# A decoder layer with two attentions and experts: maxima turned as a product into spare columns, biases added to the residual, the usual arm of the branch in line

## The reference

```python
x = layernorm(x + attn(x))          # 16 heads of 8, one shared K and V of width 8
x = layernorm(x + xattn(x, ctx))    # 16 heads of 8, 6404 keys, each head its own K and V
x = layernorm(x + ffn(x))           # 8 experts, each token takes the best one

# attn:  softmax(Q K^T / sqrt(8)) V @ Wo + bo
# xattn: scores where mask == 0 are set to -1e9, softmax, V, @ Wo^T + bo
# ffn:   probs = softmax(x @ router^T + rb); e = argmax(probs)
#        y = (x @ expert_w[e]^T + expert_b[e]) * probs[e]
```

## Time and profile before

| | us |
|---|---|
| median of 3 runs | 573.07 (571.8 to 575.85) |
| the profiled execution | 574.0 |
| its span | 572.4 |
| TensorE busy | 512.7 (90%) |
| VectorE busy | 432.6 (76%) |
| ScalarE busy | 356.1 (62%) |
| POOL busy | 186.9 (33%) |
| mean granted TensorE clock | 0.945 of full speed |

### The profile page before, as it was taken

The page is one execution under the profiler, slowest core; times in us unless marked ns, Lnnn a source line. Parts: engine busy times, 40 slices in busy tenths (PEclk is TensorE's granted clock), DMA queues, the critical chain, the costliest instruction groups (busy, mean ns, idle before and its releaser), DMA issues.

```text
span 572.4 us, 13811 instructions
## 1 busy us (share of the span) xinstructions
PE 512.7 (90%) x4112; PEld 211.0 (37%) x4120; DVE 432.6 (76%) x640; ACT 356.1 (62%) x680; POOL 186.9 (33%) x297
## 2 busy tenths in 40 slices
PE   7998899989999997857899999999999999979981
PEld 2332233323333344622344444444444444327440
DVE  5998789889999733436888888888888888302667
ACT  6147678878888863150377777777777777860210
POOL 1135798898920000010233333333333333200000
PEclk9999889999999997886999999999999999995697
DMA  3389978775000013422233111111111111110001
GB/s 85 93 298 310 306 267 300 289 272 220 11 21 11 11 50 120 137 74 56 51 65 70 43 39 36 30 36 36 32 34 36 34 36 37 34 32 24 0 0 37
DMA packets 21770, 52.56 MB, mean 92 GB/s; under 512 B 5021, under 2 KB 13375, under 8 KB 19649
## 3 DMA queue, kind: packets, MB, share of 16 engines
q1 hardware_dynamic: 19037, 22.72, 14.7%
q0 software_dynamic: 2304, 28.84, 13.8%
q10 hardware_dynamic: 356, 0.10, 0.1%
HBM read 42.10 MB, written 8.94 MB: 89 GB/s over the span
## 4 chain that ended last, share of the span: by engine, by line
PE 73%; DVE 9%; ACT 6%; issue 6%; DMA 5%; ACTq 1%; SPq 0%; DVEq 0%
PE O L1166 25%; PE ST L1387 13%; PE ST L1197 9%; PE RT L1359 8%; DMA Qs<-mxr 4%; PE RT L1183 3%; DVE mxs L718 3%; PE RT L1489 2%; PE RT L1313 2%; PE RT L1312 2%; ACT prob L1007 2%; DVE x L906 1%; ACT prob L1044 1%; PE ST L1141 1%; PE RT L1092 1%
## 5 line engine op out<-in xcount | busy, mean ns | idle before, releaser
L863 DVE TENSOR_REDUCE mxc<-RT 128x1024 f32 (+1 forms) x192 | 198.3, 1046 | 33.5 <-PE RT L1359 28.6
L1044 ACT ACTIVATE prob<-ST 128x512 f32<-128x512 f32 x320 | 172.9, 592 | 47.1 <-PE ST L1387 45.1
L718 DVE TENSOR_REDUCE mxs<-RT 128x2 f32<-128x1024 f32 x128 | 152.9, 1223 | 19.1 <-PE RT L1183 16.8
L1007 ACT ACTIVATE prob<-ST 128x512 f32<-128x512 f32 x256 | 140.3, 597 | 37.4 <-PE ST L1197 29.6
L1359 PE MATMUL RT<-Kr,Qs 64*128 64x128 f32 (+1 forms) x512 | 122.9, 380 | 8.9 <-issue 7.9
L1387 PE MATMUL ST<-Qs,Kc 64*128 64x512 f32 x320 | 123.2, 454 | 1.1 <-DMA Qs<-mxr 0.7
L1197 PE MATMUL ST<-Qs,Kself 64*128 64x512 f32 x256 | 97.1, 463 | 10.5 <-DMA Qs<-mxr 5.3
L1166 PE MATMUL O<-prob,vst 128*9 128x256 f32 x1280 | 99.1, 381 | 0.6 <-ACT prob L1044 0.6
L1183 PE MATMUL RT<-Kself,Qs 64*128 64x512 f32 x256 | 94.1, 463 | 3.4 <-DVE mxs L718 1.5
L1166 PE MATMUL O<-prob,Vs 128*9 128x256 f32 x1024 | 80.3, 386 | 2.0 <-ACT prob L1007 0.8
L1359 PEld LDWEIGHTS RT<-Kr,Qs 64*128 64x128 f32 x512 | 60.2, 186 | 38.0 <-DVE mxc L863 24.6
(11 more groups left out here) (214 smaller groups left out, 390.6 us busy)
## 6 DMA issues: line engine op xcount, KB each, us to landing
big<-in_mask POOLq DMA_DIRECT2D x16, 1760.0 KB, 7.9
big<-kd SPq DMA_DIRECT2D x66, 80.0 KB
od_s<-osb SPq DMA_DIRECT2D x14, 128.0 KB, 3.0
od_x<-osb SPq DMA_DIRECT2D x14, 128.0 KB, 1.8
Qs<-qd_s SPq DMA_DIRECT2D x12, 128.0 KB, 4.0
Qs<-qd_x SPq DMA_DIRECT2D x12, 128.0 KB, 3.8
qd_s<-Vx SPq DMA_DIRECT2D x2, 512.0 KB, 4.0
qd_x<-big SPq DMA_DIRECT2D x2, 512.0 KB, 5.0
```

The source lines that it names most:

```text
L718: v.tensor_reduce(mxs[:, h % 2, c2, :].rearrange("p (f t) -> p f t", f=2)[:, :, q], RT[r % 2][:, :].rearrange("p (f k) -> p f k", f=2), AX ...
L863: v.tensor_reduce(o, src, AX.X, ALU.max).then_inc(S("x_row_free"), 1)
L1007: nc.scalar.activation(prob[:, c % SLOTS, k * HALF:(k + 1) * HALF], ST[(2 * c + k) % 3][:, :], ACT.Exp) \
L1044: nc.scalar.activation(prob[:, b, (k % 2) * HALF:(k % 2 + 1) * HALF], ST[BANK[k]][:, :], ACT.Exp) \
```

## The change

Several edits at once. `zrow` grows from 256 to 384 columns, `clear_o` clears 384 columns of `O`, and in both attentions, but for head 0, the maxima are turned by an ordinary product with the identity that adds to these zeros in columns 256 to 383. In self-attention this moves from block 4 to the start of block 2 of the head before; the wait for the copy moves to just before the block's value products:

```diff
             def turn_max(a, h, bank):
                 pe.wait_ge(S(a + "_mx_split"), h + 1)
+                if bank is None:
+                    mmul(O[0:16, 256:256 + P], mxh[:, :, :, :].bitcast(F32).rearrange("p f k t -> p (f k t)"),
+                         ident[:, :], start=False, stop=False, skip_group_check=True).then_inc(S(a + "_mx_turned"), 1)
+                    return
...
-                mmul(O[:, 0:256], zrow[:, 0:P], zrow[:, :], start=True, stop=False, skip_group_check=True)
+                mmul(O[:, 0:256 + P], zrow[:, 0:P], zrow[:, :], start=True, stop=False, skip_group_check=True)
...
-                turn = (c + 4) % SELF_U == 0 and (c + 4) // SELF_U < HEADS
+                turn = (c + 6) % SELF_U == 0 and (c + 6) // SELF_U < HEADS
+                if turn:
+                    turn_max("s", (c + 6) // SELF_U, None)
                 self_col(c, 0)
                 if r < HEADS * SELF_U:
                     self_row(r, 1)
-                if turn:
-
-                    pe.wait_ge(S("s_exp"), 2 * c - 1)
-                    turn_max("s", (c + 4) // SELF_U, (2 * c + 1) % 3)
-                    pe.wait_ge(S("s_mx_copied"), (c + 4) // SELF_U + 1)
                 self_col(c, 1)
                 if r < HEADS * SELF_U:
                     self_row(r, 0)
+                if turn:
+                    pe.wait_ge(S("s_mx_copied"), (c + 6) // SELF_U + 1)
...
                         if turn:
-
-                            pe.wait_ge(S("x_exp"), e + 4)
-                            turn_max("x", h_turn, BANK[7])
+                            turn_max("x", h_turn, None)
                         col(g, T, 2 * b, e + max(2 * b + 1 - AGAIN[2 * b], 0))
                         if h < HEADS:
                             rows(1, b - 1, h, U)
-                        if turn:
-                            pe.wait_ge(S("x_mx_copied"), h_turn + 1)
                         col(g, T, 2 * b + 1, e + (2 * b + 2 - AGAIN[2 * b + 1]))
                         if h < HEADS:
                             rows(0, b - 1, h, U)
+                        if turn:
+                            pe.wait_ge(S("x_mx_copied"), h_turn + 1)
```

ScalarE's copies move with them: of the maxima in self-attention to block 2, in cross-attention behind exponential 5 instead of 4; of `O` in cross-attention one exponential forward:

```diff
                 step_exp(T0, 0)
-                step_exp(T0, 1)
                 if g:
                     copy_o("x", g - 1, act.snap(T0 * NBLK + NBLK))
+                step_exp(T0, 1)
...
-                    if k == 4 and g + 1 < HEADS:
-                        max_copy("x", g + 1, BANK[7])
+                    if k == 5 and g + 1 < HEADS:
+                        max_copy("x", g + 1, None)
```

```diff
+            def add_bias(a):
+
+                k = "sx".index(a) + 2
+                dve.wait_ge(S("bias_rows"), k)
+                if a == "x":
+                    dve.wait_ge(S("s_x"), QT)
+                rows = (ST[2] if a == "s" else RT[1])[:, 0:D].unsqueeze(1).to_broadcast([P, QT, D])
+                v.tensor_tensor(x[:, :, :], x[:, :, :], rows, ALU.add).then_inc(S("bias_added"), 1)
+
+            def sums_back(a):
                 dve.wait_ge(S(a + "_o_back"), 16 * 15)
                 v.reciprocal(rden[:, :], den[:, :]).then_inc(S(a + "_rden"), 1)
...
-            dve.wait_ge(S("s_pv"), HEADS * SELF_U - 2)
-            with dve.Fori(0, n1) as i:
-                keys_of_pair(1, dve.snap(i + 1))
...
+            add_bias("s")
+            sums_back("s")
+            dve.wait_ge(S("s_pv"), HEADS * SELF_U)
+            with dve.Fori(0, n1) as i:
+                keys_of_pair(1, dve.snap(i + 1))
...
             def project_out(a, w):
                 pe.wait_ge(S("sel_made"), 1)
-                warm_up(ST[2], 8)
+                if a == "x":
+                    warm_up(ST[2], 16)
...
+                pe.wait_ge(S("bias_added"), "sx".index(a) + 2)
+                if a == "s":
+                    pe.wait_ge(S("x_k_f"), n)
+                    pe.wait_ge(S("x_k_hi"), n)
...
-                    mmul(RT[1][:, q * D:(q + 1) * D], orow[:, :], bo[a][:, :], start=True, stop=False, skip_group_check=True)
-                    mm = mmul(RT[1][:, q * D:(q + 1) * D], aT[:, q * P:(q + 1) * P], w[:, :], start=False, stop=True,
-                              skip_group_check=True)
+                    mm = mmul(RT[1][:, q * D:(q + 1) * D], aT[:, q * P:(q + 1) * P], w[:, :], start=True, stop=True)
```

The expert biases are made behind unit 5 instead of unit 3, second half first; ScalarE copies them to SBUF, POOL adds them to `x`, and VectorE waits for that (`bias_in`) before unit 8 and before the statistics, in place of its two adds:

```diff
+            for h in (1, 0):
+                w = slice(4 * h, 4 * h + 4)
+                pool.wait_ge(S("bias_copied"), 2 - h)
+                if h == 0:
+                    pool.wait_ge(S("f_sum"), 4 * E)
+                g_.tensor_tensor(x[:, w, :], x[:, w, :], be_rows[h], ALU.add).then_inc(S("bias_in"), 1)
```

More of the change, by code:

```diff
@@ L177, in decoder_layer @@
         kx_hi = [kx_ha, xroom[:, 0:PAIR].bitcast(F32R)]
+        be_rows = [prob[:, 3 + h, 0:HALF].rearrange("p (t d) -> p t d", d=D) for h in range(2)]
         outs = prob[:, 2, :].rearrange("p (t d) -> p t d", d=D)
@@ L278, in o_rows @@
                     return
+                load(den[g * DH:(g + 1) * DH, :], osb[DH:P:32, g % 2, :], a + "_o_back")
                 for q in range(4 if g == HEADS - 2 else 2):
@@ L401, in _ @@
             load(we, t["we"].rearrange("d (e o) -> d e o", e=E), "we_in")
-            for q in range(QT):
+            for q in range(0, QT, 2):
                 sp.wait_ge(S("out_done"), q + 1)
@@ L898, in _ @@
             for u in range(0, 2 * QT, 2):
+                if u == QT:
+                    dve.wait_ge(S("bias_in"), 1)
                 dve.wait_ge(S("y_all"), u + 2)
@@ L911, in _ @@
             dve.wait_ge(S("f_sum"), done)
-            for h in range(2):
-                dve.wait_ge(S("y_bias"), h + 1)
-                w = slice(4 * h, 4 * h + 4)
-                ch(v.tensor_tensor(x[:, w, :], x[:, w, :], (ST[0] if h else O)[:, :]
-                                   .rearrange("p (t d) -> p t d", d=D), ALU.add))
+            dve.wait_ge(S("bias_in"), 2)
             for h in range(2):
@@ L961, in max_copy @@
                     act.wait_ge(S(f"{a}_max_in{h % 2}"), 16 * (h // 2))
-                nc.scalar.copy(mxr[:, h % 2, :], ST[bank][0:16, 0:P]).then_inc(S(a + "_mx_copied"), 1)
+                turned = O[0:16, 256:256 + P] if bank is None else ST[bank][0:16, 0:P]
+                nc.scalar.copy(mxr[:, h % 2, :], turned).then_inc(S(a + "_mx_copied"), 1)
             def copy_o(a, g, pv):
@@ L1076, in _ @@
                 nc.scalar.copy(coefT[:, h * HALF:(h + 1) * HALF], ST[1 + h][0:E, :]).then_inc(S("coefT_copied"), 1)
+            for h in (1, 0):
+                act.wait_ge(S("y_bias"), 2 - h)
+                nc.scalar.copy(be_rows[h], (ST[0] if h else O)[:, :].rearrange("p (t d) -> p t d", d=D)) \
+                    .then_inc(S("bias_copied"), 1)
             act.preload_act_table(ACT.Sqrt)
@@ L1079, in _ @@
                 std("f", h)
+            for q in range(1, QT, 2):
+                act.wait_ge(S("out_done"), q + 1)
+                act.dma_start(out.rearrange("(t p) d -> p t d", p=P)[:, q, :], outs[:, q, :]).then_inc(S("stored"), 16)
         @block.tensor
@@ L1469, in cross @@
                 values(HEADS - 1, pe.snap(n * (HEADS - 1) + n1), NBLK - 1, n * (HEADS * NCOL))
-            pe.wait_ge(S("x_q_high"), 2)
-            pe.wait_ge(S("x_q_full"), 2)
-            pe.wait_ge(S("x_q0_z"), DIRECT)
-            with pe.If(general == 1):
-                cross(True)
-            with pe.Else():
-                cross(False)
-            project_out("x", wo_x)
-            pe.wait_ge(S("x_xT_copied"), 2)
-            for q in range(QT):
-                mm = mmul(ST[0][:, q * E:(q + 1) * E], xT[:, q * P:(q + 1) * P], wr[:, :], start=True, stop=True)
@@ new lines, in finish @@
+            def finish():
+                bias_rows("x")
+                project_out("x", wo_x)
+                pe.wait_ge(S("x_xT_copied"), 2)
+                for q in range(QT):
+                    mm = mmul(ST[0][:, q * E:(q + 1) * E], xT[:, q * P:(q + 1) * P], wr[:, :], start=True, stop=True)
+                mm.then_inc(S("logits"), 1)
+                pe.wait_ge(S("we_in"), 16)
+                for u in range(2 * QT):
+                    if u >= 4:
+                        pe.wait_ge(S("f_sum"), 8 * (u // 2 - 1))
+                    q, h = 2 * (u // 4) + u % 2, (u // 2) % 2
+                    mmul(RT[h][:, (u % 2) * 512:(u % 2 + 1) * 512], xT[:, q * P:(q + 1) * P],
+                         we[:, 4 * h:4 * h + 4, :].rearrange("p e o -> p (e o)"), start=True, stop=True) \
+                        .then_inc(S("y_all"), 1)
+                    if u == 3:
+                        pe.wait_ge(S("coef"), 1)
+                        for q in range(QT):
+                            mm = nc.tensor.transpose(ST[1 + q // 4][0:E, (q % 4) * P:(q % 4 + 1) * P], lg[:, 5, q, :],
+                                                     ident[:, :])
+                        mm.then_inc(S("coefT"), 1)
+                    if u == 5:
+                        pe.wait_ge(S("coefT_copied"), 2)
+                        for q in (4, 5, 6, 7, 0, 1, 2, 3):
```

(11 more changed lines are left out.)

92 lines of the change are left out of this document (38 added, 54 removed).

## The result

The kernel after takes 524.14 us, median of 4 runs (523.77 to 524.29), against 573.9 us (571.8 to 575.85, 4 runs) on the same chip: ratio 0.9133, 95% interval 0.9097 to 0.9168. Its profiled execution took 524.29 us, span 522.6, 49.8 less than the span of before. Forecast was 527, range 517 to 541.

What follows compares the result with a forecast made beforehand. TensorE was taken to bound both stages, VectorE close behind in the first. Gains of 7.7 + 6 + 6.5 + 13.4 + 12.3 = 45.9 off 574.0 us gave 528.1, adjusted to the median 527; range 517 to 541.

Steps and rivals of the forecast that it cites:

- Turn in the self stage: Self stage: turning the maxima by a product into spare columns of O gains 8.5 us, less 0.8 for wider clearing.
- rival (a): Self stage: the earlier wait for VectorE's split binds at every turn, heads stay at 10.9 us; 538 us, chance 0.14.
- The maxima's DMA: Self stage: the DMA starts over two blocks earlier, removing the early heads' excess; 6 us, between 2 and 8.
- Cross-attention: Cross heads: turn gains 0.19 us, earlier copy of O 0.30, times 15, less 0.8 for clearing; 6.5 us.
- 0.7 for the first rows: Start of cross-attention: shorter idle time may keep the clock up for the first row units; 0.7 us of at most 2.
- The passage: Self- to cross-attention: projection 7.5 us earlier, gap at the If 5.2, first rows 0.7; sum 13.4.
- rival (b): Between the stages, without warm-up: clock stays at 1.2 GHz, products +2.5 us, query projections +1.5, rows +1; 532 us, chance 0.12.
- The gap at the If: Before cross-attention's first rows: usual arm in line and If ahead of the waits cut the 5.7 us idle time; gain 5.2.
- rival (d): Before cross-attention's first rows: the If did not cause the 5.66 us, so the gap stays; 532 us, chance 0.07.
- The end: After cross-attention: projection 8.5 us, VectorE's idle time in the experts 1.2, additions 1.4, stores 1.2; sum 12.3.
- (c): Cross-attention gives nothing, its idle time before clearing refilled by the exponential now behind the copy; 534 us, chance 0.13.
- (e): Cross-attention: moved code puts each head's inner loop across a fetch boundary, 5.7 us a head; slower, 619 us, chance 0.01.

Runs made afterwards that it cites:

- e3: Kernel after with the self stage's turn as the same product but in the old block (c + 4 instead of c + 6); 536.25 us.
- e7: Kernel after with ScalarE's copy of a cross head's sums behind the head's second exponential again; 529.35 us.
- e2: Kernel before with the turned maxima alone, in both stages, with the wider clear and the moved copies and waits of the maxima; 559.69 us.
- e1c: Kernel after with the usual arm behind the general one and the three query waits ahead of TensorE's If; 529.08 us.
- e6: Kernel after with 8 warm-up products in place of 16 ahead of the last projection; 526.13 us.
- e4: Kernel after with the one-row bias product ahead of each block's product in both projections again, and VectorE's bias addition dropped; 532.94 us.
- e9: Kernel after with the experts' bias added by VectorE out of PSUM again and all eight stores issued by SP; 527.36 us.
- e1: Kernel after with TensorE's If turned round, general arm in line and usual arm behind it, query waits still inside the arms; 523.63 us.
- e8: Kernel after with 18 warm-up products in place of 8 behind each projection; 521.81 us.
- e10: Kernel after with 18 warm-up products behind each projection and the experts' bias products split, four behind the sixth and four behind the tenth expert product; 521.61 us.

## Why the prediction was right, step by step

The time (527 for 524.14) and every stage's sum came out. Part of that is luck: in the passage and at the end, terms that were too small met losses that the prediction did not have, and two of the reasons under the numbers do not stand as given.

- **Turn in the self stage, 7.7.** Head forecast 10.4, measured 10.34: 0.59 a head where I had 0.57 less 0.05 for clearing. Clearing 384 columns records 0.34 us against 0.28 and shows in no head. That is 8.9 us. The slack of 0.2 us turned out to be nothing, as rival (a) feared, but a wait that is just met costs next to nothing (0.02 us a head by e3); rival (a) is out.
- **The maxima's DMA, 6.** 17.0 - 8.9 leaves 8.1, with 0.5 from the start: 7.6, near the upper bound of 8 that I gave for a fourth disturbed head. There was one: before, the time from clear to clear is 12.90 us at 107.20, 2.0 over an undisturbed head. e3 shows that it is the two blocks of lead, not the form of the turn.
- **Cross-attention, 6.5.** Measured 6.3 in the stage. The 14 heads from clear to clear gained 5.2 where 0.19 and 0.30 less 0.05 a head come to 6.2. The copy's term was near: 4.2 forecast for them, 3.8 by e7. The turn's was too large: 2.0 forecast, 1.2 by e2. The shorter block is not worth its full difference, since the block behind it is 0.11 us longer than before. VectorE takes the maxima without a pause there (five in 5.52 us from 385.14), which may be why; no run tests it. The other 1.1 us came ahead of the 14 heads, which is where my 0.7 for the first rows belongs: the granted clock was 1.00 from 229 to 232 us, against 0.50 from 260.3 to 264 before.
- **The passage, 13.4.** Without the 0.7 for the first rows that is 12.7, and measured are 14.0, of three terms. The projection ends 10.5 us behind the last values instead of 21.7: 11.2, not 7.5. Its products start 8.5 us behind the last values, not 9.6, and take 2.0 us where I had some 4.6, since without alternation a product takes 0.25 us and the clock had not fallen. 2.4 of it is given back: from the projection's end to the last query copy it takes 14.3 us instead of 11.9. 1.5 of that are the query products at half clock, the 1.5 that rival (b) had for them; 1.3 lie ahead of the first transposes, for which TensorE now waits on VectorE's normalisation; 0.5 comes back, as the last query copy ends closer behind the products. The gap at the If gave 5.3 for 5.2. Its cause is right in kind (rival (d) is out: e1c brings a gap back), but I took the order of the arms and the place of the waits for one thing; either one alone is enough. That e1c shows only 3.9 us of the 5.66 stays open.
- **The clock between the stages, rival (b).** It came in one of its three parts, the query products. The spread and the projection ran at 1.00 without warm-up products, and so did the first rows. At the end they did with 16, and with 8 in e6. My reason for 8.5 us there, 16 warm-ups holding the clock, is not borne out: e6 did without the second eight, though before and e2 show that eight can fail. What the traces show of the fall: in e4 at 215.1 and 491.3, 5.7 and 7.0 us behind the first spread product; before at 239.7, 7.0 behind it, but at its end within the spread. A projection that takes 2.02 us was over before the clock fell in after. By the rule of the Trainium skill, "TensorE: Matmul & The Clock Gate", Part 1, cited with rival (b), the time would have been 532; the trace has its two levels, but the fall comes later than that rival needed, for all but the query products.
- **The end, 12.3.** Measured 12.5. The projection gave 10.35 (it ends 9.03 us behind the last values, 19.38 before) for 8.5; VectorE's idle time between the experts' sums 1.78 for 1.2 (2.67 left of 3.82 and 0.63; the 0.63 is not in my sum); additions and stores 2.7 for 2.6 (e9). Together 14.8; 2.3 were given back, 1.2 in the router's products at the lower clock, most of the rest ahead of the first transposes, as in the passage.
- **The start, 0.** Measured about 0.5, within what I allowed, and no more than the same start differs by between kernels (34.4 to 35.3). **Rivals (c) and (e)** did not come: cross heads are shorter, and no inner loop shows a gap.

## What to carry to other kernels

A product that must come back through a DMA is timed by when it starts, not by how long it takes: two blocks of lead were worth as much as the shorter turn. Group products of the same kind; alternating a one-row and a full one cost 0.42 us each against 0.25. Evaluate a branch while something else still runs, ahead of the waits; then the far arm cost nothing either (e1). And look at where a copy stands in its engine's queue before rewriting the operation that waits for it.

## What was not expected of the hardware

- Eight products of 128 columns with 128 rows, or with one, take 2.02 to 2.05 us at full clock when they stand together. The same two kinds in turn take 0.41 to 0.42 us each.
- The clock held through idle times of 1.63 us (after) and 2.73 us (e6) and the products behind them; after 3.15 and 3.14 us (before, e2) it fell within the products. With 18 warm-up products ahead, the first query products ran at full clock in one profile (e8) and at half clock in another (e10).
- With the DMA engines busy for 0.97 of the time, three heads whose small load was issued 2.4 us sooner were not disturbed in after, and by at most 1.7 us in the other kernels; at 0.94 and without that lead three heads lost 7.9 us together (38.88 against 3 x 10.32).
